# Counting the first signs from PSUM, ahead of each eviction, in a top-k attention kernel

## What is computed

```
q, k = l2norm(x @ Wq), l2norm(concat(mem_k, x @ Wk));  v = concat(mem_v, x @ Wv)
dots = einsum('bhid,bhjd->bhij', q, k) * 10
dots = einsum('hg,bgij->bhij', W_pre_th, dots)        # mixes the heads
dots = where(causal, -max, dots)
vk   = top_k(dots, 64)[0][..., -1:]                   # the 64th largest of a row
attn = softmax(where(dots < vk, -max, dots))
attn = einsum('hg,bgij->bhij', W_post_th, attn)       # mixes the heads again
out  = (attn @ v * head_scale) * sigmoid(x @ Wg + bg) @ Wo
```

## Time and profile before

| | |
|---|---|
| three runs | 2096.52, 2101.4, 2099.31 us; median 2099.31 |
| profiled execution | 2098.69 us, of which the span of instructions is 2096.9 |
| TensorE, matmul running | 1952.4 us, 93% of the span |
| VectorE | 1668.8 us, 80% |
| ScalarE | 1612.7 us, 77% |
| GpSimd | 862.8 us, 41% |
| mean granted TensorE clock | 0.981 |

### The profile page before, as it was taken

How to read it: one execution, slowest core, us unless ns; L and a number is a source line. 1 busy time by engine, 2 the same in 40 slices (tenths; PEclk the granted TensorE clock), 3 DMA queues, 4 the chain that set the end, 5 groups by cost and what they waited for, 6 DMA issues and landing times. The chain is left out here.

```text
span 2096.9 us, 56133 instructions
## 1 busy us (share of the span) xinstructions
PE 1952.4 (93%) x16059; PEld 1292.3 (62%) x16060; DVE 1668.8 (80%) x7716; ACT 1612.7 (77%) x4412; POOL 862.8 (41%) x2675
## 2 busy tenths in 40 slices
PE   7996789999999999999999999999999999996997
PEld 3433456676667666766676677666766776674433
DVE  6355389978997899789978997999699969985335
ACT  4553489978997899789968996899689978963554
POOL 3000454455445544554454445544554455421000
PEclk9997899999999999999999999999999999998998
DMA  5002012301230222122211221122112211213002
GB/s 170 26 1 95 12 33 53 79 18 45 61 73 18 62 55 60 26 54 68 45 33 48 68 48 29 48 68 48 29 48 68 48 26 46 66 45 95 0 1 80
DMA packets 113228, 104.78 MB, mean 50 GB/s; under 512 B 34449, under 2 KB 110865, under 8 KB 112913
## 3 DMA queue, kind: packets, MB, share of 16 engines
q1 hardware_dynamic: 108000, 96.65, 18.6%
q10 hardware_dynamic: 4912, 4.46, 0.7%
HBM read 19.14 MB, written 12.71 MB: 15 GB/s over the span
## 5 line engine op out<-in xcount | busy, mean ns | idle before, releaser
L1076 PEld LDWEIGHTS bankC<-R,E 128*128 128x128 f32 x2560 | 319.9, 192 | 49.7 <-issue 17.6
L1060 PE MATMUL bankB<-raw,mixpre 128*128 128x76 f32 (+37 forms) x1024 | 334.5, 421 | 13.6 <-DMA raw<-SC 12.3
L1076 PE MATMUL bankC<-R,E 128*128 128x128 f32 x2560 | 333.9, 277 | 11.5 <-POOL R L1452 11.5
L1557 DVE TENSOR_SCALAR_CACHE_REDUCE S<-S,minus_thr 128x68 f32<-128x68 f32 (+56 forms) x456 | 232.9, 511 | 110.9 <-POOL minus_thr L1436 110.1
L1427 POOL TENSOR_TENSOR S<-S,diagmask 128x8 f32<-128x8 f32 x512 | 120.2, 238 | 395.4 <-ACT S L1284 360.4
L1284 ACT ACTIVATE S<-bankB,aim_first 128x68 f32<-128x68 f32 (+56 forms) x456 | 227.3, 506 | 57.8 <-PE bankB L1060 56.9
L1452 POOL TENSOR_SCALAR R<-mixpost,rinv 128x128 f32<-128x128 f32 x512 | 199.3, 402 | 101.1 <-DVE rinv L1591 99.0
L1310 ACT ACTIVATE E<-S,nmax 128x12 f32<-128x12 f32 (+56 forms) x512 | 238.8, 523 | 0.0
L1060 PEld LDWEIGHTS bankB<-raw,mixpre 128*128 128x128 f32 x1024 | 160.2, 190 | 119.0 <-issue 94.4
L1646 DVE SCALAR_TENSOR_TENSOR E<-S,limit,E 128x68 f32<-128x68 f32 (+56 forms) x456 | 221.8, 521 | 8.6 <-ACT E L1310 4.7
L1049 PE MATMUL bankD<-KT,QT 64*64 64x132 f32 (+8 forms) x2304 | 177.4, 401 | 43.3 <-ACT qk L1214 29.4
(11 more groups left out here) (187 smaller groups left out, 4188.7 us busy)
## 6 DMA issues: line engine op xcount, KB each, us to landing
X_first<-in_L_attn_x_dram ACTq DMA_DIRECT2D x8, 512.0 KB, 9.9
x<-X_first SPq DMA_DIRECT2D x8, 512.0 KB, 2.9
xt<-x SPq DMA_DIRECT2D x32, 128.0 KB, 2.4
x<-xt SPq DMA_DIRECT2D x32, 128.0 KB, 2.4
X_last<-x SPq DMA_DIRECT2D x8, 512.0 KB, 7.5
out_dram<-X_last SPq DMA_DIRECT2D x8, 512.0 KB, 2.9
raw<-SC SPq DMA_DIRECT2D x8, 258.0 KB, 5.3
raw<-SC SPq DMA_DIRECT2D x8, 254.0 KB, 4.8
```

The costliest lines, as they stand in the source:

```text
L1060: last = nc.tensor.matmul(bankB[n % 2][:, 0:wide(n)], W.mixpre[:, :], raw[n % RAWS][:, 0:wide(n)], start=True, stop=True)
L1076: last = nc.tensor.matmul(bankC[:, n % 2, jb * P:(jb + 1) * P], E[n % EBUFS][:, jb * P:(jb + 1) * P], R[n % RBUFS][:, :], start=True, stop ...
L1557: nc.vector.tensor_scalar(row, row, minus_thr[:, col(n)], None, ALU.add, ALU.max, accum_out=rmax[:, col(n)]).then_inc(max_done, 1)
```

## The change

For a ranked group the count now comes before the group's own eviction. It reads the mixed scores in `bankB` and adds the first guess itself, as the bias of the Sign. The sign is no longer turned round, so what is counted is `above`, and the slope of the table changes its sign. The count waits for the mixing (`mixed`) and not for the eviction (`S_out`). Lines that only rename `below` to `above` are left out.

```diff
@@ aim(g)
-    return -z, step / 2, -step * (counted / 2 - wanted)
+    return -z, -step / 2, -step * (counted / 2 - wanted)
@@ ScalarE
-            def count_below(n):
-                act.wait_ge(S_out, n + 1)
+            def count_above(n):
+                act.wait_ge(mixed, n + 1)
                 if ranked_upto(n - 2):
-                    act.wait_ge(below_done, ranked_upto(n - 2))
+                    act.wait_ge(above_done, ranked_upto(n - 2))
                 w = group_width(n) - IG
-                nc.scalar.activation(junk_first[n % 2][:, 0:w], S[n % SBUFS][:, 0:w], ACT.Sign, scale=-1.0,
-                                     accum_out=below[:, col(n)]).then_inc(below_done, 1)
+                nc.scalar.activation(junk_first[n % 2][:, 0:w], bankB[n % 2][:, 0:w], ACT.Sign,
+                                     bias=W.aim_first[:, group(n)],
+                                     accum_out=above[:, col(n)]).then_inc(above_done, 1)
@@ ScalarE's loop over pairs
                 if live:
+                    if is_ranked(n0):
+                        count_above(n0)
                     evict(n0)
...
                     if g == 14 and ahead:
                         score(2 * t + 2, 3)
+                    if is_ranked(n0 + 1):
+                        count_above(n0 + 1)
                     evict(n0 + 1)
-                for n in ranked_in(n0):
-                    count_below(n)
                 for n in ranked_in(n0 - 2):
                     count_sides(n)
@@ GpSimd, threshold(ns)
-                pool.wait_ge(below_done, ranked_upto(ns[-1]))
-                nc.gpsimd.tensor_tensor(moved[:, cols], below[:, cols], W.aim_slope[:, steps],
+                pool.wait_ge(above_done, ranked_upto(ns[-1]))
+                nc.gpsimd.tensor_tensor(moved[:, cols], above[:, cols], W.aim_slope[:, steps],
                                         ALU.mult).then_inc(thr_moved, len(ns))
```

More of the change, by code:

```diff
@@ L764, in attention_phase @@
         minus_thr = sb("minus_thr", [P, RING])
-        below = sb("below", [P, RING])
+        above = sb("above", [P, RING])
         signs = sb("signs", [P, RING])
@@ L799, in attention_phase @@
         masked = sem("masked")
-        below_done = sem("below_done")
+        above_done = sem("above_done")
         thr_moved = sem("thr_moved")
```

## The result

| | before | after |
|---|---|---|
| median of 6 runs | 2099.14 us (2096.52 to 2101.4) | 2113.59 us (2110.75 to 2116.15) |
| profiled execution, its span | 2098.69, 2096.9 | 2110.75, 2109.0 |
| TensorE, VectorE, ScalarE busy | 1952.4, 1668.8, 1612.7 us | 1956.3, 1670.4, 1629.9 us |

The changed kernel is slower: ratio 1.007, 95% interval 1.0059 to 1.0082, so 14.5 us. The forecast was 2115. The profiled execution of after is the fastest of its six, 12.1 us above the one of before.

A forecast was written before the change was run, and what follows sets the result against it. TensorE bounds the first three tiles, sharing the fourth with VectorE; what decides is how soon ScalarE hands back bank D. Six terms sum to 2.0 us a batch, 16 for eight: 2098.7 + 16 = 2115 us, range 2101 to 2124.

The forecast's parts named there:

- The price of a count, 0.06: ScalarE: a count reading PSUM with a bias from a tile costs 0.06 us more than before, bounds 0 to 0.16.
- 27 us more work on ScalarE, nearly all beside TensorE's: ScalarE: 456 counts at 0.06 add 27 us, nearly all beside TensorE's work, ScalarE being busy 176.01 of 205.86 us a batch.
- Pairs 16, 17 and 24: Copy of xT (16, 24) and score copy (17) come one count later: exposed 0.46, 0.14 and 0.33 us a batch.
- Pair 9: Score copy without slack comes one count later, less 0.08 us that ScalarE stood idle: 0.29 us a batch.
- Pair 8: TensorE waits for R, which is behind the later threshold: 0.3 us a batch; the later copy of xT is hidden behind it.
- Pair 27, 0.49: Score copy ahead of the last four columns comes one count later, 0.61 less 0.12 us of ScalarE idle time: 0.49 a batch.
- Bank B, nothing: Bank B stays occupied up to two counts longer before the next pair's mixing: costed at nothing; if exposed at pair 8, 0.4 us.
- The threshold: GpSimd's second mask now stands between second eviction and threshold: 0.3 us later when ScalarE is saturated, exposed through R at pair 8.
- Nothing comes through: Rival: TensorE regains lost time at its next wait; 2099 us, or 2103 if a quarter comes through. Nothing or little: chance 0.14.
- The threshold wins: Rival: counting first uses ScalarE's idle time and brings R forward, so 11.5 us of waits go: 2088 us. Chance 0.08.
- Slower still: Rival: the threshold path bounds the wide tiles, pairs 26 and 27 add 5 us: 2120, or 2125 with dearer counts. Chance 0.18.
- The change doesn't do what it says: Rival: reading PSUM is so cheap that the count shrinks; at no extra price 2112 us, within the forecast, no separate chance.

The follow-up runs named there:

- experiment 4: Changed kernel with the copy of xT moved ahead of the first count and eviction in the pair that opens a tile: 2104.04 us, ratio 1.0024 to the kernel before.
- experiment 5: Changed kernel with the old count order and SBUF source in the first two pairs of each tile only: 2104.98 us, ratio 1.003 to the kernel before.
- experiment 8: Kernel before plus eight Sign counts of 508 columns behind the last tile, from SBUF and PSUM, with and without a bias: 2098.57 us in one run.
- Experiment 2: Changed kernel with both PSUM counts put back behind both evictions, the next mixing waiting for them: 2104.97 us, ratio 1.0033 to the kernel before.
- experiment 7: Kernel before with each first count given a bias of zero from a tile, nothing else changed: 2106.76 us, ratio 1.0039.
- experiment 3: Changed kernel with GpSimd making the threshold ahead of the mask of the pair's second group: 2112.05 us, ratio 1.007 to the kernel before.
- Experiment 9: Changed kernel with old count order and source in the third pair of each tile only (10, 18, 26): 2117.28 us, ratio 1.0088 to the kernel before.
- experiment 1: Kernel before with each count right behind its own group's eviction, still from SBUF without a bias: 2129.22 us, ratio 1.0148.

## Why the prediction was right, and where it was not

**What bounds the kernel.** Right in the main. A delay of ScalarE counts where TensorE waits for bank D, and a little where it waits for R. The list of TensorE's idle times left out the 12.3 us of waits for the raw rows. Moving three copies a batch past the count took back 9.7 of 14.5 us (experiment 4), two pairs in eight carried 8 (experiment 5).

**The price of a count, 0.06.** Right: 0.06 by experiment 8, and 0.45 against 0.46 in pair 16. It was read off the eviction's row as a whole. That it is made of +0.10 and -0.04 could not be seen there.

**"27 us more work on ScalarE, nearly all beside TensorE's".** This step was wrong, and it is the larger miss in understanding. Experiment 2 has that price without the new order and costs 6.9 us; experiment 7, with 0.09 a count, costs 8. The reason given was a share, ScalarE busy 176.01 of 205.86 us, where each place had to be looked at. The prediction followed what stands between the two evictions, and not what stands behind the counts in the same pair, where the counts had always been: the score copies that TensorE needs at pairs 11, 14, 15, 19 and 25 in experiments 2 and 7. The trace of before has one of them as a wait of 0.28 us (the row in experiment 7), and a wait for ScalarE says that the queue ahead of the copy is exposed. In after itself these copies are felt at pairs 14 and 15 alone. At 19 and 25 nothing is lost there, and the 0.10 at pair 11 is R's (experiment 3).

**Pairs 16, 17 and 24.** Right to about 0.01: 0.45, 0.13 and 0.34 against 0.46, 0.14 and 0.33. The slack between the end of a copy and TensorE's use, less 0.14, did hold.

**Pair 9.** 0.17 where 0.29 was forecast. The place was right and one term mis-sized. ScalarE in pair 9 of after:
```profile
1106.61 0.38 ACT L1294 ACTIVATE junk_first<-bankB,aim_first 128x148 bf16<-128x148 f32 x1
...
1106.96 0.40 ACT L1284 ACTIVATE S<-bankB,aim_first 128x156 f32<-128x156 f32 x1
1107.24 0.60 ACT L1273 COPY SC<-bankD 128x520 f32<-128x520 f32 x1
```
The eviction's step is 0.28 us when the copy behind it need not wait. In the earlier trace rows it is 0.47, so the slack was 0.19 and not 0.08: the prediction took the count from start to start, but the idle time from the eviction's end. The count's 0.35 less 0.19 is 0.16, which is what arrived.

**Pair 8.** The size was right, 0.27 against 0.3, by luck: the mechanism was right only in part. All of it was to be R, held up by the threshold behind the second mask, with the copy of xT hidden behind it. GpSimd, ScalarE and TensorE there in after:
```profile
1100.17 0.75 POOL L1455 TENSOR_SCALAR R<-mixpost,rinv 128x128 f32<-128x128 f32 x2
```
```profile
1100.80 0.40 ACT L1200 COPY xnT<-bankD 128x256 f32<-128x256 f32 x1
```
```profile
1101.34 1.10 PE L1008 MATMUL bankD<-Wq,xnT 128*128 128x512 f32 x2
```
From the start of pair 7's mixing (1092.71 in before, 1097.11 in after) R starts after 2.91 and 3.06 us, so 0.15 later and not 0.3. The copy of xT ends at 1101.20 and the q projection starts 0.14 behind it, which is the distance of no slack: it is not hidden. With the copy first, 0.15 of the 0.27 remain (experiment 4). So about 0.15 is R and 0.12 the copy. With the counts behind both evictions, 0.13 to 0.18 remain as well (experiments 2 and 7), so the dearer counts alone can delay R by about as much. How much of R's 0.15 is the mask no run says, since in experiment 3 the mask is still ahead of R.

**Pair 27, 0.49.** This term failed: 0.06. The prediction took ScalarE's 0.12 of idle time before pair 27's own copy, but not the 0.43 before the copy of pair 26. The 0.12 was too small as well: from start to start the eviction takes 0.73 us there in the earlier trace rows and 0.51 in after, so the slack was 0.22 and the term should have been 0.39. A moved step is not only late for what it is now ahead of; it is also gone from where it was, and if idle time lay before its new place, all that follows comes earlier. Experiment 9 took that gift away, and 0.33 to 0.49 was lost in four of the batches.

**Bank B, nothing.** Right for the change. TensorE now does wait at the narrowest place, pair 8, for 0.2 to 0.7 us in five of the other batches and 0.21 in this one, but there it waits for R right after, as the prediction said. With the counts behind both evictions TensorE waits 3.0 us more for the counts themselves (experiment 2).

**The threshold.** VectorE's wait for it grew, from 110.1 to 119.1 us, but experiment 3 shows that this costs nothing. By way of R it costs the 0.10 at pair 11 and some part of the 0.15 at pair 8.

**The sum.** 1.75 in the batch against 2.0, and 14.5 us against 16. It was closer than its terms: 0.43 too much at pair 27, 0.12 at pair 9 and 0.03 at pair 8 were in part made up by 0.33 at pairs 11, 14 and 15, which had been put at nothing. That the time came so close is partly luck, since misses of opposite sign met.

**The rivals.** "Nothing comes through" fell: what a batch has lost by pair 26 it has still lost at its end. "The threshold wins" fell with R's 11.7 us against 11.5. "Slower still" fell: the fourth tile grew by 0.37, and TensorE's places explain it. "The change doesn't do what it says" was half true in a way that I had not set apart: PSUM does shrink the count, by 0.04, and the pointer takes it back.

## What to carry to other kernels

Before calling more work on an engine "hidden", go through the waits of the bounding engine and see what stands in the queue ahead of each thing it waits for: every instruction there can be exposed at full price, however low the share of busy time. Take slack and price in the same way, both from start to start. Of a moved step, cost both ends: what it now delays, and what comes earlier where it was, above all if there was idle time in front of its new place. And compare orders only after the one urgent item (here the copy of xT) stands first, since otherwise it is the item and not the order that is measured; with it first and the bias taken from the evictions, the new order was the fastest of all twelve.

## What was not expected of the hardware

A count that reads what the eviction ahead of it wrote, and waits for its semaphore, started 0.50 us after it, where the copy of xT, which does neither, started after 0.37 (268 columns). No run tells the reading from the wait. That 0.13 is the likely reason, argued and not shown by itself, why a cheaper count made the slowest of all kernels. And TensorE's clock fell to 1.2 GHz in the midst of the attention phase, behind single idle times of 1.0 to 1.5 us. At pair 8 it cost a batch 1.7 us more (experiment 1, and after). It happened in after as well, in one batch of the profiled execution:
```profile
683.75 0.86 PE L1076 MATMUL bankC<-R,E 128*128 128x128 f32 x4 [1.02 <-POOL R L1455]
684.49 5.37 PE L1008 MATMUL bankD<-Wq,xnT 128*128 128x512 f32 x8
```
The projection takes 5.37 us where the same one in other batches takes 3.67, and the window from 684 to 690 us has a mean granted clock of 0.72. The same idle time of 1.02 ahead of the same matmuls in the batch of the rows did not bring it on; what decides between them stays open. It is one more way in which a short delay can cost more than itself, and it makes the loss of a kernel near such an idle time less sure than its steps.
